# A fused attention and feed-forward kernel: TensorE's large products are placed between the bursts of small scan products

## The reference, cut to what matters

```python
def _rwkv6_forward(x, ...):                      # x: (2, 4096, 512), 16 heads of 32
    sx = concat([zeros, x[:, :-1]]) - x
    m = tanh((x + sx * time_maa_x) @ tm_w1).reshape(B, T, 5, 32)
    mix = time_maa_wkvrg + einsum('btfa,fac->btfc', m, tm_w2)
    xw, xk, xv, xr, xg = [x + sx * mix[:, :, i] for i in range(5)]
    r, k, v = xr @ Wr, xk @ Wk, xv @ Wv
    g = silu(xg @ Wg)
    w = exp(-exp(time_decay + tanh(xw @ td_w1) @ td_w2))
    def step(state, rkvw):                       # per head, over 4096 steps
        a = k_t[..., :, None] * v_t[..., None, :]
        y = einsum('bhk,bhkv->bhv', r_t, state + u * a)
        return w_t[..., :, None] * state + a, y
    yn = per_head_layernorm(y) * ln_w + ln_b
    return (yn * g) @ Wo

h = layernorm(x) * (1 + ca) + sa;  x = x + ga * attention(h)
h = layernorm(x) * (1 + cb) + sb;  x = x + gb * ffn(h)     # FP4-quantised gate, up, down
```

## Time and profile before

| | us |
|---|---|
| median of 3 runs | 4354.51 |
| lowest, highest | 4353.13, 4363.64 |
| span of the profiled execution | 4344.3 |
| TensorE products busy | 3769.6 (87%) |
| VectorE busy | 3500.5 (81%) |
| ScalarE busy | 1612.9 (37%) |
| GpSimd busy | 1139.1 (26%) |

### The profile page before, as it was taken

One profiled execution on the slowest core, in us unless ns is written; L12 is line 12 of the kernel. 1 busy time (PEld: TensorE's weight loads), 2 busy tenths in 40 slices (PEclk: granted clock), 3 DMA queues, 4 the chain that ended last, 5 costly groups with the idle time before them and its releaser, 6 DMA issues. The chain is left out here.

```text
span 4344.3 us, 155632 instructions
## 1 busy us (share of the span) xinstructions
PE 3769.6 (87%) x65992; PEld 2590.6 (60%) x65992; DVE 3500.5 (81%) x7798; ACT 1612.9 (37%) x3173; POOL 1139.1 (26%) x736
## 2 busy tenths in 40 slices
PE   4888898888898888888888874399999999999999
PEld 3767777676677766777767652145454545545454
DVE  4777788777688776778777757799999999999997
ACT  2434434344353443443434313233333333333333
POOL 1121112211212212112121104433333333333332
PEclk7999999999899998999999986599999999999999
DMA  3000000000000000000000011001111111111100
GB/s 112 13 22 27 23 28 18 23 27 18 23 27 23 27 22 19 27 18 33 18 23 27 13 71 66 15 23 37 31 37 35 33 38 30 37 32 36 38 30 30
DMA packets 73617, 133.45 MB, mean 31 GB/s; under 512 B 13248, under 2 KB 14016, under 8 KB 72896
## 3 DMA queue, kind: packets, MB, share of 16 engines
q1 hardware_dynamic: 72896, 123.13, 8.8%
HBM read 89.56 MB, written 33.55 MB: 28 GB/s over the span
## 5 line engine op out<-in xcount | busy, mean ns | idle before, releaser
L747 POOL TENSOR_TENSOR raw_up<-raw_up,raw_gate 128x1024 f32<-128x1024 f32 x128 | 309.8, 2420 | 1184.1 <-DVE raw_up L797 1184.1
L915 DVE COPY_PREDICATED Am<-pick,banks 128x64 f32<-128x64 uint8 (+2 forms) x1792 | 460.6, 257 | 128.3 <-DVE Am L915 12.6
L1630 PE MATMUL fbank<-dT,hqT 128*128 128x512 f16 x2112 | 490.3, 381 | 21.1 <-ACT hqT L1547 21.1
L1618 PE MATMUL fbank<-gT,xqT 128*128 128x464 f16 (+1 forms) x2304 | 490.1, 363 | 11.4 <-issue 6.6
L1618 PE MATMUL fbank<-uT,xqT 128*128 128x464 f16 (+1 forms) x2304 | 488.3, 362 | 0.0
L526 PE MATMUL banks<-raw_up,raw_gate 128*128 128x256 f32 x2048 | 465.8, 386 | 6.2 <-issue 4.4
L526 PEld LDWEIGHTS banks<-raw_up,raw_gate 128*128 128x128 f32 x2048 | 391.0, 193 | 61.0 <-issue 7.0
L758 POOL TENSOR_TENSOR yrs<-yvar,neg_half 128x32 f32<-128x32 f32 x32 | 174.0, 5437 | 846.0 <-DVE yvar L944 846.0
L1618 PEld LDWEIGHTS fbank<-gT,xqT 128*128 128x128 f16 x2304 | 225.3, 98 | 247.7 <-issue 11.5
L1558 ACT ACTIVATE sil<-fbank,und 128x464 f32<-128x464 f32 (+1 forms) x192 | 124.0, 646 | 656.0 <-PE fbank L1618 656.0
L1618 PEld LDWEIGHTS fbank<-uT,xqT 128*128 128x128 f16 x2304 | 225.6, 98 | 231.7 <-issue 1.3
(11 more groups left out here) (235 smaller groups left out, 8063.1 us busy)
## 6 DMA issues: line engine op xcount, KB each, us to landing
raw_scale<-in_L_attn_x SPq DMA_DIRECT2D x32, 512.0 KB, 3.8
xres<-in_L_attn_x SPq DMA_DIRECT2D x32, 512.0 KB, 3.5
x_after_attention<-xres SPq DMA_DIRECT2D x32, 512.0 KB, 3.6
xl<-x_after_attention SPq DMA_DIRECT2D x64, 256.0 KB, 2.7
xr<-x_after_attention SPq DMA_DIRECT2D x64, 256.0 KB, 2.7
out<-xr SPq DMA_DIRECT2D x64, 256.0 KB, 2.0
raw_gate<-in_L_ffn_w_gate SPq DMA_DIRECT2D x1, 2816.0 KB, 11.5
raw_up<-in_L_ffn_w_up SPq DMA_DIRECT2D x1, 2816.0 KB, 18.7
```

Of the source, the lines that this page charges most:

```text
L747: nc.gpsimd.tensor_tensor(xf[:, j % NXF].rearrange("p g b t -> p (g b) t"), xf[:, j % NXF].rearrange("p g b t -> p (g b) t"), hT[:, :, :, ...
L915: nc.vector.copy_predicated(dst, mask, src).then_inc((done or A_step).sem, 1)
L1618: last = nc.tensor.matmul(GU[2 * pair + t][:, 0:w], xqT[:, u, a, g, :], W[:, b_, g, lo_:hi_], start=(k == 0), stop=(k == 3 * G - 1))
L1630: last = nc.tensor.matmul(DN[1 - u][:], hqT[:, a, kk, :], dT[:, b_, kk, :], start=(first and kk == 0), stop=(end and kk == KF - 1))
```

## The change

The score products and the outer products become two functions, `pe_scores` and `pe_outer`. At the end of a body only the scores of the next chunk's piece 0 are made; its outer products move to the start of the next body, behind the first group of g. `pe_g` makes one group (four calls) at a time and stands at n = 0, 1, 2 and 3 instead of two groups at n = 1 and 2. td1 moves from n = 3 to n = 4, `pe_wo` of batch 0 from n = 4 to n = 5 and 6 (two calls each), `pe_wo` of batch 1 from n = 6 to n = 7. All of them, and td2, now stand between the outer products of piece n and the output products of piece n - 1. On ScalarE the stacking of j = 4 moves from the end of a body to the next one, between the two copies of g. On VectorE `dve_z` moves from n = 1 to n = 0 and `dve_out` of batch 0 from n = 5 to n = 6, behind `dve_ww`.

```diff
         def pe_scores(pe, c, n):
...
+
+        def pe_outer(pe, c, n):
+            b, q = divmod(n, Q)
+            sc = SC[n % 2]
             if n == 0:
                 settled_after(pe, mod_done, (vT_done, c), (kT_done, c))
             for g in range(G):
...
-        def pe_g(pe, c, h, do_p):
-            if h == 0:
+        def pe_g(pe, c, g, do_p):
+            if g == 0:
                 xf_wait(pe, c, NMIX - 1)
                 after(pe, x1_done, c - 2)
                 if do_p:
                     after(pe, mf_done, c + 1)
-            else:
+            elif g == 2:
                 after(pe, gu_done, c, 1)
-            for g in (2 * h, 2 * h + 1):
-                for k in range(G):
-                    last = nc.tensor.matmul(SMALL[:, (g % 2) * BT:(g % 2 + 1) * BT], w_g[:, k, g * P:(g + 1) * P],
-                                            xf[:, NMIX - 1, k].rearrange("p b t -> p (b t)"), start=(k == 0), stop=(k == G - 1))
-            last.then_inc(proj_done.sem, 1)
-
-        def pe_wo(pe, f, b, fenced, gated):
-            after(pe, z_done, f)
-            if b == 0 and fenced:
-                after(pe, u1_done, f + 2)
-            elif b == 0 and gated:
-                after(pe, gu_done, f + 1)
-            if b == 1:
-                after(pe, x1_done, f, 1)
             for k in range(G):
+                last = nc.tensor.matmul(SMALL[:, (g % 2) * BT:(g % 2 + 1) * BT], w_g[:, k, g * P:(g + 1) * P],
+                                        xf[:, NMIX - 1, k].rearrange("p b t -> p (b t)"), start=(k == 0), stop=(k == G - 1))
+            if g % 2:
+                last.then_inc(proj_done.sem, 1)
+
+        def pe_wo(pe, f, b, ks, fenced, gated):
+            if ks[0] == 0:
+                after(pe, z_done, f)
+                if b == 0 and fenced:
+                    after(pe, u1_done, f + 2)
+                elif b == 0 and gated:
+                    after(pe, gu_done, f + 1)
+                if b == 1:
+                    after(pe, x1_done, f, 1)
+            for k in ks:
                 last = nc.tensor.matmul(SMALL[:], yn[:, k, b, :], w_o[:, b, k, :], start=(k == 0), stop=(k == G - 1))
-            last.then_inc(wo_done.sem, 1)
+            if ks[-1] == G - 1:
+                last.then_inc(wo_done.sem, 1)
 
         def pe_body(pe, i, do_p, do_w, do_f, more, more2):
             c, f = i - 1, i - 2
+            if do_w:
+                pe_g(pe, c, 0, do_p)
+                pe_outer(pe, c, 0)
             for n in range(1, 8):
                 if do_w:
                     pe_scores(pe, c, n)
-                    if n <= 2:
-                        pe_g(pe, c, n - 1, do_p)
+                    pe_outer(pe, c, n)
+                    if n <= 3:
+                        pe_g(pe, c, n, do_p)
+                if n == 4 and do_p:
+                    pe_td1(pe, i)
+                if n == 5 and do_f:
+                    pe_wo(pe, f, 0, (0, 1), do_p, do_w)
+                if n == 6 and do_f:
+                    pe_wo(pe, f, 0, (2, 3), do_p, do_w)
+                if n == 6 and do_p:
+                    pe_td2(pe, i)
+                if n == 7 and do_f:
+                    pe_wo(pe, f, 1, (0, 1, 2, 3), do_p, do_w)
+                if do_w:
                     pe_y(pe, c, n - 1)
-                if n == 3 and do_p:
-                    pe_td1(pe, i)
                 if n <= 5 and do_p:
                     pe_delta(pe, i, n - 1)
-                if n == 4 and do_f:
-                    pe_wo(pe, f, 0, do_p, do_w)
-                if n == 6 and do_p:
-                    pe_td2(pe, i)
-                if n == 6 and do_f:
-                    pe_wo(pe, f, 1, do_p, do_w)
...
-        def act_stack(act, i):
-            after(act, mf_done, i)
-            after(act, m_done, i)
-            after(act, delta_done, i - 1)
-            for j in range(NMIX):
+        def act_stack(act, i, js):
+            if js[0] == 0:
+                after(act, mf_done, i)
+                after(act, m_done, i)
+                after(act, delta_done, i - 1)
+            for j in js:
...
             if do_w:
                 act_gu(act, c, 0)
+            if do_p:
+                act_stack(act, i, (4,))
+            if do_w:
                 act_gu(act, c, 1)
...
             if more:
-                act_stack(act, i + 1)
+                act_stack(act, i + 1, (0, 1, 2, 3))
...
-                if n == 1 and do_f:
+                if n == 0 and do_f:
                     dve_z(dve, f)
...
-                if n == 5 and do_f:
-                    dve_out(dve, f, 0)
                 if n == 6 and do_p:
                     dve_ww(dve, i)
+                if n == 6 and do_f:
+                    dve_out(dve, f, 0)
```

More of the change, by code:

```diff
@@ L1042, in _ @@
                 act_m(act, 0)
-                act_stack(act, 0)
+                act_stack(act, 0, (0, 1, 2, 3))
                 run(act, act_body)
```

## The result

| | before | after |
|---|---|---|
| median of the runs, us | 4353.82 | 4220.02 |
| lowest, highest | 4350.05, 4363.64 | 4212.4, 4230.55 |
| span of the profiled execution | 4344.3 | 4210.4 |

The ratio is 0.9706, 95% interval 0.9675 to 0.9738: 134 us less, where 48 were forecast.

What follows compares the result with a forecast made beforehand. VectorE's chain and TensorE's were taken to alternate; a chunk was 78.2 - 9.38 (VectorE's waits) + 3.5 + 3.75 = 76.1, with 0.55 of remaining waits 76.6 us, giving 4306.5 us. The range was 4245 to 4375.

Steps and rivals of the forecast that it cites:

- second rival: TensorE's gaps stay and TensorE sets the chunk: 78.2 us, no change, 4354 us; chance 0.17.
- step (1): g in four pieces, first ahead of outer(0): fills TensorE's waits for k's transpose (0.75 us a chunk) and gu (0.47).
- Step (2): Scan bursts broken by a large product: gaps shrink but don't vanish, between none and today's 8.6 us a chunk left.
- Step (3): z at n = 0, stacking of j = 4 behind g's first half: VectorE saves its 0.76 us wait.
- Step (4): wo(0) at n = 5 and 6, wo(1) at n = 7: waits at A(5), A(7) go; wo(1) waits for out(0), adding 3.75 us.
- the leg: From A(7) to the projections: projection starts 4.4 us behind A(7) instead of 0.65, 3.75 us that nothing covers.
- Step (5): VectorE's s_tmp waits for GpSimd's addition after each mix: all three additions met, 3.5 us a chunk come back.
- fewer additions: Rival: VectorE meets fewer of GpSimd's additions, half of (5), no wait remains: chunk 74.3 us, 4238 us; chance 0.15.
- the gaps stay: The second rival: TensorE's gaps remain and it sets the chunk, no change, 4354 us; chance 0.17.
- the new waits ahead of td2 and wo(1): Rival: TensorE's waits for mix(4) and out(0), up to 3 us each, cost clock; two stretches give 4409 us; chance 0.13.

Runs made afterwards that it cites:

- g_in_two: The changed kernel with g made in halves at n = 1 and 2 again and the first outer products right behind the first scores: 4283.3 us.
- y_adjacent: The changed kernel with y(n-1) right behind the outer products of piece n again, the large product behind y: 4312.8 us, 0.990 of before.
- wo_back: The changed kernel with wo(0) whole at n = 4, wo(1) at n = 6 and out(0) at n = 5 again: 4205.0 us, 0.9656 of before.
- small_add_after: The changed kernel with GpSimd adding one column of each 128 instead of all: 4225.9 us.
- around_outer: The changed kernel with wo(0) at n = 5, wo(1) at n = 6, each large product of n = 1 to 5 halved around outer(n): 4174.7 us, 0.9586 of before.

## Why the prediction was wrong

**The bound** is where it failed. I made the sum on VectorE's chain (78.2 less its waits, plus what comes back) and took TensorE's gaps and clock as something that VectorE may or may not see. In the changed kernel TensorE waits 2.6 us in 28 chunks for another engine, and taking 87 us of work from VectorE changes nothing. The rows read beforehand pointed there: in the earlier trace rows TensorE waits 34 us for other engines, 1.2 a chunk, while in the earlier trace rows VectorE waits 262.7. TensorE's own stream sets the chunk: 64.5 us of products, 8.3 of gaps, 1.7 for half clock. The one sum I made on that side, in the second rival (77.0 when the gaps stay), left the clock at its old value. The gaps did stay, and the chunk was 74.5; had I put 3.4 us of half clock in place of 10.4 in that line, it would have given 73.5. (A small slip of reading besides: the 29.4 us from the projections to A(0) are not without a gap. TensorE is busy throughout the first 25.2; then it waits 0.75 for the transpose of k, which step (1) counts, and in the shown chunk it stands once more from 1373.84 on, 0.6 us of it before A(0).)

**Step (1), g in pieces:** both waits (0.75 and 0.47) went, as worked out. g_in_two shows that the pieces are worth more, 1.9 us a chunk, through gaps and clock.

**Step (2), breaking the bursts:** right that transfers of code cause the gaps and that a burst of 256 instructions does not avoid them; wrong that the gaps shrink. Not seen: that nearly the same sum of gaps, still in bursts of small products, keeps the clock when large products stand between shorter bursts. Counted in the clock records (a stretch that begins in the gap or at most 2 us behind it): in the kernel before, 54 of 74 gaps of 1.5 us or more had a stretch at half clock behind them, in the kernel after 21 of 59; of those of 1 to 1.5 us it was 8 of 48 before, 17 of 50 in y_adjacent and 3 of 67 after. Nor is it only that the longest gaps have gone: of the gaps of 1.5 to 2.2 us it was 43 of 63 before, 37 of 64 in y_adjacent and 19 of 56 after. This is the term that the sum lacked, 3.5 us a chunk by the account and 3.0 by the places at full clock. What exactly decides whether a gap costs clock stays open.

**Step (3), z early:** VectorE's wait went. Its value was put at 0.76 us for the wrong reason; it is 1.4 us a chunk through gu and g.

**Step (4), wo behind outer:** the leg was right, and beside the point. The projection starts 4.2 us (median) after A(7), where 4.4 were worked out. From A(7) to the next A(0) I had 3.75 us more than before; the mean over 28 chunks went from 31.0 to 34.3, 3.2 more. From A(0) to A(7) I had 41 and 0.55 of waits, and it is 40.2. But wo_back shows that the order as a whole gained nothing.

**Step (5), GpSimd's addition:** the term that was mis-sized within the sum, +3.5 us. s_tmp's mean over the 28 chunks is 641 ns (row below), 8 x (0.641 - 0.28) = 2.9 us a chunk, so +0.9; the 2.6 us too much are 78 of the 86 us between 4306 and 4220. Whoever corrects it alone gets the right time by luck, from the wrong bound: small_add_after takes the whole term away and gains nothing. The cause is the race told below.

```profile
L926 DVE TENSOR_TENSOR s_tmp<-state,T 128x128 f32<-128x128 f32 x224 | 143.6, 641 | 0.0
```

**The rivals:** "fewer additions" (4238) was nearest in time, and true of the additions, but it too reckons on VectorE's chain, so its nearness is luck; "the gaps stay" was true of the gaps; the new waits ahead of td2 and wo(1) hardly came (2.6 us in all at L558), nor did the loss of clock that they were to bring. The rule of "Runtime: NRT & Kernel Launch" in the Trainium skill, "Instruction fetch mechanics", that refilling is hidden, is contradicted here: the gaps grow by 3.3 us with 512 more instructions in the bursts and by 0.6 with the same ones elsewhere. Its block of 16 KiB agrees with 8.81 MB in 538.

## What to carry to other kernels

When two engines hand work to one another, write the chunk as a sum on each of them, with the clock as a term of its own, and ask which engine has waits with another's name: the one without any is the bound. Bursts of small products used up code faster than it arrived here, so spread large products between them and count the run that is left on both sides of each; the gaps may keep their sum and still cost less clock. A step moved on an engine that is not the bound can matter through a buffer that it frees for the one that is.

## What the runs showed that was not expected

Two instructions on different engines that hold each other up can race, and hundredths of a microsecond decide. VectorE's s_tmp and GpSimd's addition after the same mix, twice in the timeline of after (GpSimd's rows, then VectorE's):

```profile
1338.54 2.18 POOL L764 TENSOR_TENSOR raw_up<-raw_up,raw_gate 128x1024 f32<-128x1024 f32 x1 [3.31 <-DVE raw_up L814]
...
1352.26 2.35 POOL L764 TENSOR_TENSOR raw_up<-raw_up,raw_gate 128x1024 f32<-128x1024 f32 x1 [4.34 <-DVE raw_up L814]
```

```profile
1338.88 1.99 DVE L926 TENSOR_TENSOR s_tmp<-state,T 128x128 f32<-128x128 f32 x1
...
1352.29 0.28 DVE L926 TENSOR_TENSOR s_tmp<-state,T 128x128 f32<-128x128 f32 x1
```

Where s_tmp starts 0.03 us behind the addition, it runs in 0.28 and the addition takes 2.35 instead of 2.18; where it starts 0.34 behind, it waits out the addition. At n = 4, over 28 chunks of each kernel, the 34 starts up to 0.036 us behind the addition were short, and those from 0.047 us on waited for what was left of it. So a VectorE that is not late often slips in at n = 4 and n = 6 (15 of 28 each), and only n = 5, where g's product lies between, collides nearly always (26 of 28). At n = 6 one start at 0.036 us was long too, so the border lies there. Whether it is a rule was not tried.

Small products cost more beside large ones: a set of 16 calls of 32x32x16 is 0.21 us in a burst and 0.43 in the tail by the account (0.27 and 0.46 by the places at full clock), and the products of a chunk, taken at the places at full clock, grow from 63.9 us before to 64.8 after and 65.4 in around_outer without one more product.
